# Value products behind the first query block's scores, in a causal attention with a mixture of experts behind it

## The chip, the core and the metric

One core of a Trainium2 chip runs one kernel. The metric is the device time of one execution in microseconds (us). The engines run side by side, each through its own list of instructions in order, and wait for one another on semaphores: TensorE (matmuls, PE in the profile, its weight loads PEld), VectorE (DVE), ScalarE (ACT), GpSimd (POOL) and SyncE (SP), which here only issues the DMAs.

## What is computed

The input x has 16 batches of 256 tokens with 128 features. Two layers follow each other, each added to its input:

```
x = x + attention(layernorm(x))     # 16 heads, keys of 8, values of 64, causal softmax
x = x + experts(layernorm(x))       # 8 experts, 64 tokens of each batch per expert
q = (x @ Wq), k = (x @ Wk), v = (x @ Wv);  scores = q k^T / sqrt(8), masked above the diagonal
ctx = softmax(scores) @ v;  attention = ctx @ Wo
probs = softmax(x @ gate_w); each expert takes its top 64 tokens: gelu(xin @ w1) @ w2, weighted, added back
```

All is float32. Where the kernel needs products close to float32 accuracy, it splits a factor into a rounded part ("hi") and a rest ("lo") and adds three faster products: hi x hi, hi x lo and lo x hi. `split_product` does this.

## The kernel before

The kernel has two stages, one after the other: `attention` and `experts`. The change is in `attention` alone.

Attention works in 64 units, u = 4b + j: batch b (16) times group j of four heads (4). I call j the unit of its batch, 0 to 3. Each engine has a function `batch(b, par)` with a loop over j, and in each pass of it the engine works on several units at different stages, so that the pass of unit u holds, on TensorE:

- L513, L515: the scores s1 of the second query block (tokens 128 to 255) of unit u+1, with the causal mask added by a matmul;
- L530, L531: eight transposes of the normalized probabilities of unit u-1 into the PSUM buffers t_ps, half f = 0 and half f = 1;
- L548: sixteen context matmuls of unit u-2 into ctx_ps, half as wide in the output's partitions as the others;
- L558: the value product of unit u+2 (three matmuls, L494 to L496), a quarter of the batch's values, into a buffer misc_ps;
- L565: four transposes of the last third of unit u-1's probabilities;
- L571, L572: the scores s0 of the first query block (tokens 0 to 127) of unit u+2;
- L584: the query and key products of unit u+3 (six matmuls, L494 to L496) into the other misc_ps buffer;
- then, into the misc_ps buffer that the value product used, one of four pieces of other work: the transposes of the normalized input xn1 (j = 0, L595), those of the second layer's xn2 (j = 1, L601), half of the output projection (j = 2, L606; its other half stands at L519 in unit 3), the gate's logits (j = 3, L610). Ahead of it TensorE waits for `v_ready`, ScalarE's copy of the value product out of that buffer (L591).

ScalarE copies the query and key product (L313, qk_hi), computes the exponentials of s0 (L317) and s1 (L330) with `exps`, four instructions each, and copies t_ps to probT (L323 for half 0, L341 for half 1) and the value product to v_sb (L337). VectorE makes qT and kT from qk_hi and the product (L409, L412), the negated maxima of s1 (L417) and s0 (L458), copies (L446, L479), the reciprocals, and the two layer normalizations: L394, called at L450 in unit 0 (xn1 of batch b+1) and at L455 in unit 1 (xn2 of batch b-2), two instructions of 128 tokens each. GpSimd spreads kT over four blocks of a diagonal (L266, `k_diag`, on which both score products wait through `k_ready`) and multiplies the probabilities by the reciprocal sums (L258 first query block, L281 second); in units 0 and 3 it has two small operations of the normalizations between L266 and L281 (L270 to L277).

The order of the work is written out by hand: it is the order of the `if` blocks in each engine's loop. There is no scheduler. `batches` writes the first and the last batches out and runs the middle ones in a loop.

Of the kernel before, what the change touches and what calls it, by code (L numbers as in the profile page):

```python
# [10 lines left out]
ACT = mybir.ActivationFunctionType  # L11
# [68 lines left out]
def attention(nc, x_tiles, w_q, w_k, w_v, w_o, gate_w, w1, w2,  # L80
# [5 lines left out]
    with ExitStack() as ctx:  # L86
# [201 lines left out]
        @block.scalar  # L288
        def _(act):

            act.wait_ge(wqk_loaded, 32)
            for w in range(2):
                nc.scalar.activation(wqk_hi[:, w, :, :, :],
                                     bcast(wqk_raw[:, w, :].rearrange("p (h d) -> p h d", h=H), 2, 4),
                                     ACT.Copy, scale=(DK ** -0.5 if w == 0 else 1.0)).then_inc(w_hi, 1)
            act.wait_ge(wv_loaded, 16)
            nc.scalar.activation(wv_hi[:, :], wv_raw[:, :], ACT.Copy).then_inc(w_hi, 1)

            def exps(r, block_, scores, keys, first, done):
                for i in range(HG):  # L300
                    last = nc.scalar.activation(  # L301
                        prob[r][:, first + i * keys:first + (i + 1) * keys], scores[:, i, :], ACT.Exp,
                        bias=neg_max[:, r, block_, i:i + 1], accum_out=sums[:, r, block_, i:i + 1])
                last.then_inc(done, 1)

            def batch(b, par):
                for j in range(G):
                    u = b * G + j
                    r1, r2, rm = (j + 1) % RING, j % RING, (j + 1) % RING
                    if has(u + 2, UNITS):  # L310
                        act.wait_ge(qk_done, u + 3)
                        await_count(act, qk_ready, u + 1)
                        nc.scalar.activation(qk_hi[r2][:, :, :],  # L313
                                             misc_ps[(3 * j) % 2][:, :].rearrange("p (a t) -> p a t", a=2),
                                             ACT.Copy).then_inc(qk_hi_done, 1)
                    if has(u + 1, UNITS):
                        act.wait_ge(max0, u + 2)  # L317
                        await_count(act, normed, u * 2)
                        exps(r1, 0, s0_ps, P, 0, exp0)
                    if has(u - 1, UNITS):  # L320
                        act.wait_ge(t_done, (u - 1) * 3 + 1)
                        await_count(act, ctx_done, u - 2)
                        nc.scalar.activation(probT[rm][:, 0:512], t_ps[rm][:, :], ACT.Copy).then_inc(t_act, 1)  # L323
                    if j == 1 and has(b + 1, B):
                        act.wait_ge(xT_done, b + 2)
                        nc.scalar.activation(xT_hi[1 - par][:, :], misc_ps[(3 * j + 1) % 2][:, 0:T],
                                             ACT.Copy).then_inc(xT_hi_done, 1)
                    if has(u + 1, UNITS):
                        act.wait_ge(max1, u + 2)
                        exps(r1, 1, s1_ps, T, HG * P, exp1)  # L330
                    if has(u + 2, UNITS):
                        w, q = u + 2, (j + 2) % G
                        vb = par if j < 2 else 1 - par
                        act.wait_ge(v_done, w + 1)

                        await_count(act, ctx_done, w - q - G)
                        nc.scalar.activation(v_sb[vb][:, q % 2, (q // 2) * 512:(q // 2 + 1) * 512],  # L337
                                             misc_ps[(3 * j) % 2][:, :], ACT.Copy).then_inc(v_ready, 1)
                    if has(u - 1, UNITS):
                        act.wait_ge(t_done, (u - 1) * 3 + 2)  # L340
                        nc.scalar.activation(probT[rm][:, 512:1024], t_ps[1 - rm][:, :], ACT.Copy).then_inc(t_act, 1)  # L341
                    if j == 2 and has(b - 2, B):
                        act.wait_ge(xn2_ready, b - 1)
                        nc.scalar.activation(xg_hi[:, bass.ds((b - 2) * TB, TB), :], xn2[:, :, :],
                                             ACT.Copy).then_inc(xg_hi_done, 1)

            batches(act, batch)
# [139 lines left out]
        def _(pe):  # L487
# [17 lines left out]
            def batch(b, par):  # L505
                for j in range(G):
# [26 lines left out]
                    if has(u - 2, UNITS):  # L533
# [15 lines left out]
                                                            v_sb[vb][:, kb, h * DV:(h + 1) * DV], rhs,  # L549
                                                            start=(kb == 0), stop=(kb == 1))  # L550
                        last.then_inc(ctx_done, 1)
                    if has(u + 2, UNITS):
                        w, q = u + 2, (j + 2) % G
                        xb = par if j < 2 else 1 - par
                        pe.wait_ge(qk_ready, w + 1)
                        toks = slice((q % 2) * P, (q % 2 + 1) * P)
                        cols = slice((q // 2) * 512, (q // 2 + 1) * 512)
                        split_product(misc_ps[(3 * j) % 2][:, :], xT_hi[xb][:, toks], xT_lo[xb][:, toks],  # L558
                                      wv_hi[:, cols], wv_lo[:, cols]).then_inc(v_done, 1)
                    if has(u - 1, UNITS):  # L560
                        w = u - 1
                        pe.wait_ge(t_act, w * 2 + 1)
# [4 lines left out]
                    if has(u + 2, UNITS):  # L567

                        pe.wait_ge(k_ready, u + 3)
                        await_count(pe, exp0, u + 2)  # L570
                        nc.tensor.matmul(s0_ps[:, :, :], qT[r2][:, 0:P], k_diag[r2][:, :, 0:P], start=True, stop=False)  # L571
                        nc.tensor.matmul(s0_ps[:, :, :], ident_bf[:, :], bcast(causal[:, :], 1, HG),  # L572
                                         start=False, stop=True).then_inc(s0_done, 1)
                    if has(u + 3, UNITS):
                        w, g = u + 3, (j + 3) % G
                        xb = par if j < 1 else 1 - par
                        heads = slice(g * HG, (g + 1) * HG)
                        qk_ps = misc_ps[(3 * j + 1) % 2]
                        pe.wait_ge(xT_ready, b + 1 if j < 1 else b + 2)

                        await_count(pe, *[(gate_ready, b - 2), (xT_ready, b + 2 if has(b + 1, B) else B), (x2T_ready, b - 1),
                                          (x1_ready, b)][j])
                        for a in range(2):
                            last = split_product(qk_ps[:, a * T:(a + 1) * T],  # L584
                                                 wqk_hi[:, a, heads, :, :].rearrange("p h r d -> p (h r d)"),
                                                 wqk_lo[:, a, heads, :, :].rearrange("p h r d -> p (h r d)"),
                                                 xT_hi[xb][:, :], xT_lo[xb][:, :])
                        last.then_inc(qk_done, 1)
# [361 lines left out]
```

## Time and profile before

| | us |
|---|---|
| median of 3 runs | 674.44 (673.14 to 677.0) |
| the profiled execution | 672.88 |
| its span, first to last instruction | 671.0 |
| TensorE busy | 591.7 (88%) |
| VectorE busy | 437.2 (65%) |
| ScalarE busy | 418.8 (62%) |
| GpSimd busy | 363.5 (54%) |

In the page's forty slices of the span (16.8 us each) TensorE is busy for nine tenths or more from the third to the twenty-sixth slice, which is attention; behind it come the routing and the experts, where TensorE has a gap and is then full again. The granted TensorE clock is 0.966 of full speed over the span, and full speed in the batches between 80 and 450 us. The DMA queues move 12.26 MB, most of it at the start and in the second stage. Busy times are sums of instruction times; a pipelined matmul's time overlaps the next one's, so distances between starts say more than durations there.

### The profile page before, as it was taken

To read this page: it belongs to the slowest core of one execution; us is meant where nothing else is said; L and a number is where in the kernel's file an instruction comes from. 1 tells how busy PE (TensorE), PEld (TensorE's weight loads), DVE (VectorE), ACT (ScalarE), POOL (GpSimd) and SP (SyncE) were. 2 spreads that over 40 slices of the span, in tenths; PEclk is the share of its full clock that TensorE was granted. 3 is DMA by queue.
4 is the path that set the end of the run, shared out by engine and by line. 5 is a ranking of instruction groups with operands and counts; after the bars stand their busy time and mean duration, and the time that the engine had idled before them with its cause. 6 is when DMAs were issued, how large, how long until landed. Compare 5 with 4: busy or idle time off the path is not lost. (4 is left out here: it accounts for less than half of the span.)

```text
span 671.0 us, 14745 instructions
## 1 busy us (share of the span) xinstructions
PE 591.7 (88%) x4996; PEld 482.5 (72%) x4996; DVE 437.2 (65%) x1072; ACT 418.8 (62%) x1418; POOL 363.5 (54%) x290
## 2 busy tenths in 40 slices
PE   1799999999999999999999999988408999999964
PEld 0467777878778777787877877766407989989863
DVE  3678787787887878878778787774475234433233
ACT  2699778787787877878778787773205443323320
POOL 1688778687776867768777687763240110111120
PEclk9999999999999999999999999999758999999995
DMA  9500000000000000000000000000001001000001
GB/s 275 172 1 1 2 1 1 1 3 1 1 0 0 0 0 0 0 0 0 0 0 0 0 0 1 1 0 2 0 32 48 17 18 31 11 17 18 17 17 40
DMA packets 13547, 12.26 MB, mean 18 GB/s; under 512 B 832, under 2 KB 10304, under 8 KB 13504
## 3 DMA queue, kind: packets, MB, share of 16 engines
q1 hardware_dynamic: 13504, 11.69, 5.9%
q8 instruction: 27, 0.44, 0.3%
q14 instruction: 16, 0.13, 0.1%
HBM read 9.57 MB, written 2.11 MB: 17 GB/s over the span
## 5 line engine op out<-in xcount | busy, mean ns | idle before, releaser
L301 ACT ACTIVATE prob<-s_ps,neg_max 128x128 f32<-128x128 f32 (+1 forms) x512 | 209.7, 433 | 36.4 <-DVE neg_max L417 20.4
L266 POOL TENSOR_TENSOR k_diag<-kT,own_block 128x1024 fp32r<-128x1024 f32 x64 | 121.3, 1895 | 111.0 <-DVE kT L412 111.0
L281 POOL TENSOR_TENSOR probn<-prob,inv 128x1024 f32<-128x1024 f32 x64 | 121.3, 1896 | 2.6 <-DVE inv L482 2.6
L301 ACT ACTIVATION_READ_ACCUMULATOR prob<-s_ps,neg_max 128x1 f32 x512 | 111.8, 218 | 0.0
L548 PE MATMUL ctx_ps<-probT,v_sb 128*64 128x256 f32 (+1 forms) x1024 | 97.3, 332 | 0.9 <-DVE probT L479 0.9
L737 POOL TENSOR_TENSOR y_parts<-y_sb,y_parts 128x512 fp32r<-128x512 f32 x16 | 20.9, 1306 | 140.4 <-ACT y_parts L753 140.4
L548 PEld LDWEIGHTS ctx_ps<-probT,v_sb 128*64 128x64 f32 x1024 | 63.6, 136 | 29.9 <-issue 11.6
L417 DVE TENSOR_REDUCE neg_max<-s_ps 128x4 f32<-128x1024 f32 x64 | 77.9, 1217 | 0.4 <-PE s_ps L515 0.4
L458 DVE TENSOR_REDUCE neg_max<-s_ps 128x4 f32<-128x512 f32 x64 | 44.1, 688 | 48.4 <-PE s_ps L572 48.4
L258 POOL TENSOR_TENSOR probn<-prob,inv 128x512 f32<-128x512 f32 x64 | 66.7, 1042 | 4.4 <-PE t_ps L565 4.1
L847 DVE TENSOR_TENSOR y_sb<-y_ps,slot_prob 128x512 f32<-128x512 f32 x16 | 11.1, 692 | 88.5 <-PE y_ps L925 88.5
L446 DVE COPY ctxT<-ctx_ps 128x512 f32<-128x512 f32 x64 | 43.9, 685 | 33.9 <-PE ctx_ps L548 32.8
L323 ACT ACTIVATE probT<-t_ps 128x512 f32<-128x512 f32 x64 | 39.1, 610 | 40.4 <-PE t_ps L531 40.4
L501 PE MATMUL misc_ps<-wo_sb,ctxT 128*128 128x128 f32 x512 | 63.8, 280 | 0.6 <-DVE xn2T L432 0.6
L530 PE MATMUL t_ps<-ident,probn 128*128 128x128 f32 x256 | 60.7, 277 | 1.4 <-DVE probT L479 1.0
L501 PEld LDWEIGHTS misc_ps<-wo_sb,ctxT 128*128 128x128 f32 x512 | 61.4, 196 | 0.8 <-issue 0.8
L531 PE MATMUL t_ps<-ident,probn 128*128 128x128 f32 x256 | 59.7, 273 | 0.0
L925 PE MATMUL y_ps<-w_sb,w_raw 128*64 128x128 f32 x1024 | 59.4, 274 | 0.0
L925 PEld LDWEIGHTS y_ps<-w_sb,w_raw 128*64 128x64 f32 x1024 | 55.6, 137 | 2.1
L761 ACT ACTIVATE xin_hi<-pick_hi_ps 128x512 fp32r<-128x512 f32 x16 | 9.6, 599 | 72.5 <-PE pick_lo_ps L884 72.5
L772 ACT ACTIVATE w_raw<-h_ps 128x512 f32<-128x512 f32 x64 | 38.2, 599 | 26.0 <-PE h_ps L905 23.7
L513 PE MATMUL s_ps<-k_diag,qT 128*128 128x512 f32 x128 | 53.0, 473 | 0.5 <-ACT v_sb L337 0.5
(127 smaller groups left out, 1403.6 us busy)
## 6 DMA issues: line engine op xcount, KB each, us to landing
x_all<-in_L_attn_x SPq DMA_DIRECT2D x4, 512.0 KB, 6.9
w_raw<-in_L_ffn_w SPq DMA_DIRECT2D x1, 2048.0 KB, 11.2
toks<-tok_rows SPq DMA_DIRECT2D x8, 256.0 KB, 3.1
out<-x_all SPq DMA_DIRECT2D x16, 128.0 KB, 1.8
wv_raw<-in_L_attn_Wv SPq DMA_DIRECT2D x1, 512.0 KB, 4.7
wo_sb<-in_L_attn_Wo SPq DMA_DIRECT2D x1, 512.0 KB, 5.8
wqk_raw<-in_L_attn_Wq SPq DMA_DIRECT2D x1, 64.0 KB, 3.5
wqk_raw<-in_L_attn_Wk SPq DMA_DIRECT2D x1, 64.0 KB, 3.5
```

The costliest lines, as they stand in the source:

```text
L258: nc.gpsimd.tensor_tensor(probn[r][:, 0:HG * P].rearrange("p (i k) -> p i k", i=HG), prob[r][:, 0:HG * P].rearrange("p (i k) -> p i k", i=HG),
L266: nc.gpsimd.tensor_tensor(k_diag[r][:, :, :], bcast(f32(kT[r][:, :]), 1, HG), bcast(own_block[:, :], 2, T), ALU.mult).then_inc(k_ready, 1)
L281: nc.gpsimd.tensor_tensor(probn[r][:, HG * P:].rearrange("p (i k) -> p i k", i=HG), prob[r][:, HG * P:].rearrange("p (i k) -> p i k", i=HG ...
L301: last = nc.scalar.activation(prob[r][:, first + i * keys:first + (i + 1) * keys], scores[:, i, :], ACT.Exp, bias=neg_max[:, r, block_, i: ...
L417: nc.vector.tensor_reduce(out=neg_max[:, r1, 1, :], in_=s1_ps[:, :, :], axis=AX.X, op=ALU.max, negate=True).then_inc(max1, 1)
L458: nc.vector.tensor_reduce(out=neg_max[:, r2, 0, :], in_=s0_ps[:, :, :], axis=AX.X, op=ALU.max, negate=True).then_inc(max0, 1)
L501: last = nc.tensor.matmul(to[:, tb * D:(tb + 1) * D], context[:, c, tb * P:(tb + 1) * P], wo_sb[:, c, :], start=(c == 0), stop=(c == chunk ...
L513: nc.tensor.matmul(s1_ps[:, i:i + 2, :], qT[r1][:, P:T], k_diag[r1][:, i:i + 2, :], start=True, stop=False)
L530: nc.tensor.transpose(t[:, i, 0:P], q0[:, 2 * f + i, :], ident[:, :])
L531: last = nc.tensor.transpose(t[:, i, P:T], q1[:, 2 * f + i, 0:P], ident[:, :])
L548: last = nc.tensor.matmul(ctx_ps[half * DV:(half + 1) * DV, pair, kb * P:T], v_sb[vb][:, kb, h * DV:(h + 1) * DV], rhs, start=(kb == 0), s ...
L925: last = nc.tensor.matmul(y_ps[half * CAP:(half + 1) * CAP, q, :], hT[m % RING][:, half, c, q * CAP:(q + 1) * CAP], w2_sb[:, 2 * (m % EP) ...
```

## The change

In TensorE's loop, the block with the value product moves behind two others: the four transposes L565 and the scores s0. It then stands directly ahead of the query and key products. In ScalarE's loop, the copy of t_ps half 1 into probT moves ahead of the copy of the value product. The semaphores and their counts stay as they are; VectorE, GpSimd and the DMAs are not touched.

```
 ScalarE, in batch():
                         exps(r1, 1, s1_ps, T, HG * P, exp1)
+                    if has(u - 1, UNITS):
+                        act.wait_ge(t_done, (u - 1) * 3 + 2)
+                        nc.scalar.activation(probT[rm][:, 512:1024], t_ps[1 - rm][:, :], ACT.Copy).then_inc(t_act, 1)
                     if has(u + 2, UNITS):
...
                         nc.scalar.activation(v_sb[vb][:, q % 2, (q // 2) * 512:(q // 2 + 1) * 512],
                                              misc_ps[(3 * j) % 2][:, :], ACT.Copy).then_inc(v_ready, 1)
-                    if has(u - 1, UNITS):
-                        act.wait_ge(t_done, (u - 1) * 3 + 2)
-                        nc.scalar.activation(probT[rm][:, 512:1024], t_ps[1 - rm][:, :], ACT.Copy).then_inc(t_act, 1)
 TensorE, in batch():
                         last.then_inc(ctx_done, 1)
+                    if has(u - 1, UNITS):
...
+                            last = nc.tensor.transpose(t[:, i, :], q1[:, i, P:T], ident[:, :])
+                        last.then_inc(t_done, 1)
+                    if has(u + 2, UNITS):
+
+                        pe.wait_ge(k_ready, u + 3)
+                        await_count(pe, exp0, u + 2)
+                        nc.tensor.matmul(s0_ps[:, :, :], qT[r2][:, 0:P], k_diag[r2][:, :, 0:P], start=True, stop=False)
+                        nc.tensor.matmul(s0_ps[:, :, :], ident_bf[:, :], bcast(causal[:, :], 1, HG),
+                                         start=False, stop=True).then_inc(s0_done, 1)
                     if has(u + 2, UNITS):
                         w, q = u + 2, (j + 2) % G
...
                         split_product(misc_ps[(3 * j) % 2][:, :], xT_hi[xb][:, toks], xT_lo[xb][:, toks],
                                       wv_hi[:, cols], wv_lo[:, cols]).then_inc(v_done, 1)
-                    if has(u - 1, UNITS):
...
-                        pe.wait_ge(k_ready, u + 3)
...
```

TensorE before, one pass in a unit 0, from the last context matmuls on (`wv`, `xT` into misc_ps0 is the value product, `ident`, `probn` the transposes, `k_diag`, `qT` and `causal` the scores s0, `wqk` the query and key products, `xn1` the work that reuses misc_ps0):

```order
L548 MATMUL ctx_ps<-probT0,v_sb0 64x128 x2
L494 MATMUL misc_ps0<-wv_hi,xT_hi1 128x512
L495 MATMUL misc_ps0<-wv_lo,xT_hi1 128x512
L496 MATMUL misc_ps0<-wv_hi,xT_lo1 128x512
L565 MATMUL t_ps1<-ident,probn1 128x128 x4
L571 MATMUL s0_ps<-k_diag0,qT0 128x512
L572 MATMUL s0_ps<-causal,ident_bf 128x512
L494 MATMUL misc_ps1<-xT_hi1,wqk_hi 128x256
L495 MATMUL misc_ps1<-xT_lo1,wqk_hi 128x256
```

The same place of the changed kernel, in which L557 is what L565 was, and L563 and L564 are what L571 and L572 were:

```order
L548 MATMUL ctx_ps<-probT0,v_sb0 64x128 x2
L557 MATMUL t_ps1<-ident,probn1 128x128 x4
L563 MATMUL s0_ps<-k_diag0,qT0 128x512
L564 MATMUL s0_ps<-causal,ident_bf 128x512
L494 MATMUL misc_ps0<-wv_hi,xT_hi1 128x512
L495 MATMUL misc_ps0<-wv_lo,xT_hi1 128x512
L496 MATMUL misc_ps0<-wv_hi,xT_lo1 128x512
L494 MATMUL misc_ps1<-xT_hi1,wqk_hi 128x256
L495 MATMUL misc_ps1<-xT_lo1,wqk_hi 128x256
```

The three value matmuls have moved past six others and stand last but one group ahead of the work that reuses their buffer.

ScalarE before, one pass from the exponentials of s1 on:

```order
L301 ACTIVATE prob1,sums<-s1_ps,neg_max 128x256 x4
L337 ACTIVATE v_sb0<-misc_ps0 128x512
L341 ACTIVATE probT1<-t_ps0 128x512
L313 ACTIVATE qk_hi1<-misc_ps1 128x512
L301 ACTIVATE prob0,sums<-s0_ps,neg_max 128x128 x4
```

The same place of the changed kernel (L333 is what L341 was, L340 what L337 was):

```order
L301 ACTIVATE prob1,sums<-s1_ps,neg_max 128x256 x4
L333 ACTIVATE probT1<-t_ps0 128x512
L340 ACTIVATE v_sb0<-misc_ps0 128x512
L313 ACTIVATE qk_hi1<-misc_ps1 128x512
L301 ACTIVATE prob0,sums<-s0_ps,neg_max 128x128 x4
```

The two copies have changed places; what stands around them is as before.

## Rows read from the trace of the kernel before

**Rows 1.** Busy time (instructions) by engine in one batch; then clock, DMA share, GB/s.

```profile
299.59:327.53 27.94, 27.20 (x214) 21.52 (x214) 22.20 (x55) 22.16 (x83) 20.69 (x16) 1.00 0.00 0
```

**Rows 2.** TensorE's waits, 50 to 450 us: us in total, times, longest.

```profile
PE misc_ps L601 <- issue: 5.5, 7, 0.8
PE misc_ps L601 <- DVE xn L394: 4.6, 6, 0.8
```

**Rows 3.** Timeline of TensorE, unit 3: start, us, engine, line, what, number.

```profile
324.76 0.50 PE L494 MATMUL misc_ps<-wv_hi,xT_hi 128*128 128x512 f32 x1
...
325.33 0.40 PE L496 MATMUL misc_ps<-wv_hi,xT_lo 128*128 128x512 f32 x1
...
325.56 0.60 PE L565 MATMUL t_ps<-ident,probn 128*128 128x128 f32 x4
...
327.05 0.28 PE L496 MATMUL misc_ps<-xT_hi,wqk_lo 128*128 128x256 f32 x1
...
327.17 0.51 PE L610 MATMUL misc_ps<-gate_sb,xn2T 128*128 128x8 f32 x4
```

**Rows 4.** Timeline of ScalarE in the same unit.

```profile
325.76 0.60 ACT L337 ACTIVATE v_sb<-misc_ps 128x512 f32<-128x512 f32 x1 [0.36 <-PE misc_ps L496]
...
327.45 0.60 ACT L313 ACTIVATE qk_hi<-misc_ps 128x512 fp32r<-128x512 f32 x1 [0.60 <-PE misc_ps L496]
```

**Rows 5.** Timeline of several engines in an early unit.

```profile
25.80 0.61 ACT L337 ACTIVATE v_sb<-misc_ps 128x512 f32<-128x512 f32 x1
...
26.32 0.60 ACT L313 ACTIVATE qk_hi<-misc_ps 128x512 fp32r<-128x512 f32 x1
...
26.46 0.49 PE L513 MATMUL s_ps<-k_diag,qT 128*128 128x512 f32 x1 [0.18 <-ACT v_sb L337]
...
26.95 0.48 DVE L409 SCALAR_TENSOR_TENSOR qT<-qk_hi,minus_low,misc_ps 128x256 fp32r<-128x256 f32 x1 [0.56 <-ACT qk_hi L313]
...
27.91 1.89 POOL L266 TENSOR_TENSOR k_diag<-kT,own_block 128x1024 fp32r<-128x1024 f32 x1 [1.18 <-DVE kT L412]
```

**Rows 6.** Timeline of GpSimd, VectorE and TensorE, unit 0.

```profile
329.59 1.90 POOL L266 TENSOR_TENSOR k_diag<-kT,own_block 128x1024 fp32r<-128x1024 f32 x1 [2.31 <-DVE kT L412]
...
331.49 0.59 DVE L394 TENSOR_SCALAR xn<-x_all,mv,rstd 128x128 f32 x2
...
332.37 1.90 POOL L281 TENSOR_TENSOR probn<-prob,inv 128x1024 f32<-128x1024 f32 x1
...
333.24 0.43 PE L595 MATMUL misc_ps<-ident,xn 128*128 128x128 f32 x2
```

**Rows 7.** The same engines in unit 1.

```profile
337.07 1.90 POOL L281 TENSOR_TENSOR probn<-prob,inv 128x1024 f32<-128x1024 f32 x1
...
337.61 2.44 DVE L394 TENSOR_SCALAR xn<-x_all,mv,rstd 128x128 f32 x2
...
338.93 1.04 POOL L258 TENSOR_TENSOR probn<-prob,inv 128x512 f32<-128x512 f32 x1
...
340.15 0.41 PE L601 MATMUL misc_ps<-ident,xn 128*128 128x128 f32 x2 [0.79 <-issue]
```

**Rows 8.** VectorE and GpSimd in the experts' stage.

```profile
645.82 0.35 DVE L853 TENSOR_SCALAR place<-col_no,slot_tok 128x256 fp32r<-128x256 bf16 x1
...
645.86 1.43 POOL L737 TENSOR_TENSOR y_parts<-y_sb,y_parts 128x512 fp32r<-128x512 f32 x1 [5.26 <-ACT y_parts L753]
```

**Rows 9.** GpSimd and TensorE in unit 2.

```profile
342.17 1.90 POOL L266 TENSOR_TENSOR k_diag<-kT,own_block 128x1024 fp32r<-128x1024 f32 x1 [2.20 <-DVE kT L412]
...
344.70 0.47 PE L571 MATMUL s_ps<-k_diag,qT 128*128 128x512 f32 x1
```

**Rows 10.** TensorE in the first units.

```profile
18.87 0.79 PE L571 MATMUL s_ps<-k_diag,qT 128*128 128x512 f32 x1 [0.32 <-POOL k_diag L266]
...
24.85 0.50 PE L571 MATMUL s_ps<-k_diag,qT 128*128 128x512 f32 x1 [1.01 <-POOL k_diag L266]
...
31.88 0.41 PE L595 MATMUL misc_ps<-ident,xn 128*128 128x128 f32 x2 [0.58 <-DVE xn L394]
```

More of the change, by code:

```diff
@@ L551, in batch @@
                         last.then_inc(ctx_done, 1)
[L552 to L559, printed above, removed]
                     if has(u - 1, UNITS):
@@ L573, in batch @@
                                          start=False, stop=True).then_inc(s0_done, 1)
+                    if has(u + 2, UNITS):
+                        w, q = u + 2, (j + 2) % G
+                        xb = par if j < 2 else 1 - par
+                        pe.wait_ge(qk_ready, w + 1)
+                        toks = slice((q % 2) * P, (q % 2 + 1) * P)
+                        cols = slice((q // 2) * 512, (q // 2 + 1) * 512)
+                        split_product(misc_ps[(3 * j) % 2][:, :], xT_hi[xb][:, toks], xT_lo[xb][:, toks],
+                                      wv_hi[:, cols], wv_lo[:, cols]).then_inc(v_done, 1)
                     if has(u + 3, UNITS):
```

## Prediction

> **What bounds the kernel now.** I read the windows first, then TensorE's waits, then the timeline of one batch on all engines. Attention fills the first two thirds of the span, and in its middle every batch takes the same 27.9 us. In one such batch TensorE is busy for 27.20 of 27.94 us and no other engine for more than 22.2 [rows 1]. The reader is to see that TensorE streams nearly without a gap: what is added to its order, or makes it wait, lengthens the batch. Its waits between 50 and 450 us come to about 11 us, and nearly all of that is one place, L601, the transpose of xn2 in unit 1 of a batch: 5.5 + 4.6 us over 13 batches, 0.78 each [rows 2]. So at most 10 us can be won by ordering; the other places have no wait to remove.
>
> Why L601 waits decides much here. VectorE's two L394 instructions of unit 1 take 2.44 us from 337.61, where the two of unit 0 take 0.59 [rows 6, 7]. They run beside GpSimd's L281 and L258. The pair ends 0.08 us behind the end of L258 (338.93 + 1.04 = 339.97; 337.61 + 2.44 = 340.05), the transpose follows at 340.15 [rows 7]. A normalization that starts once a large GpSimd product has started waits for the whole product. In unit 0 the pair falls into the gap between k_diag's end and L281, in which GpSimd has only the two small operations from L275 on, so it is free [rows 6].
>
> **The change, part by part.** TensorE's instructions are the same in number; only their order changes. VectorE and GpSimd keep theirs, and no DMA moves.
>
> *The first scores come earlier.* A value product costs TensorE 0.23 us per instruction (325.33 to 325.56), so 0.7 for three [rows 3]. Transposes and s0 now start 0.7 to 0.8 us earlier, if the keys are ready. VectorE's maximum L458, which waits for s0, and all queued behind it come forward. In unit 3 that queue is what makes qT late, and k_diag with it: qk_hi starts at 327.45 and k_diag at 329.59, 2.14 us later [rows 4, 6]. Where VectorE was free, qT started 0.63 behind qk_hi (26.32 to 26.95) and k_diag 0.96 behind qT (27.91) [rows 5]. With the queue gone I take these: k_diag at 327.45 + 0.63 + 0.96 = 329.04 instead of 329.59, and L281, 2.78 behind it (329.59 to 332.37 [rows 6]), at 331.82 instead of 332.37. By itself that is no gain: it keeps TensorE from waiting at s0, which it now reaches 0.7 us earlier.
>
> *The value product comes late for its copy.* At the end of each unit TensorE waits for v_ready before it writes to the misc_ps buffer that the value product used. From the start of the last value matmul: it ends 0.40 later, the copy starts 0.03 behind (325.33 + 0.40 = 325.73, copy at 325.76 [rows 3, 4]), takes 0.60, and TensorE reacts 0.05 later (copy 25.80 + 0.61 = 26.41, matmul at 26.46 [rows 5]): 1.08 us. TensorE itself now has only the q/k product in between: 0.23 and six steps of 0.12 (327.05 to 327.17 [rows 3]), 0.94. So it waits 0.14, say 0.15, at the end of units 0, 2 and 3; before, transposes and s0 filled 0.7 us more and it had no such wait. In unit 1 it lies under the L601 wait. The swap on ScalarE costs nothing: the second transposed half was done long before, and the value copy couldn't start any sooner than the product ends. If ScalarE came out of the exponentials late, the wait would grow by up to the 0.60 of the copy that now stands ahead; I take 0.15, bounds 0 and 0.75.
>
> *The normalization of unit 0 loses its gap.* This term decides. The 0.15 at the end of unit 3 pushes TensorE's context product of unit 0 and with it VectorE's L394 pair from 331.49 to 331.64. A free tile alone takes about 0.35 (as L853's [rows 8]) and the pair 0.59, so the second starts some 0.25 behind the first, at 331.89. L281 now starts at 331.82, 0.07 earlier. What happens at such distances: an L853 started 0.04 before an L737 (645.82 and 645.86) ran free in its usual 0.35 and the GpSimd product took 1.43 [rows 8]; the second L394 of unit 1 starts 0.05 behind L258 and waits all of it [rows 7]. The border lies between 0.04 ahead and 0.05 behind; my 0.07 behind is on the wrong side by little. Blocked, the tile is ready at 331.82 + 1.90 + 0.08 = 333.80, and the transpose L595 starts at 333.90 instead of 333.24: +0.65.
>
> The Trainium skill, SBUF — State Buffer, section "Who interferes with whom", says that issue order decides who gets the port pair shared by VectorE and GpSimd, and that the other blocks fully. The waits of rows 7 agree with it. By that rule the border is at equal starts, which makes the blocked case a little likelier than the rows alone do; had the two engines shared the port instead, the tile would be late by tenths and this term would be near nothing.
>
> *Units 1 and 2 behind it.* From the end of the normalization to the next k_diag is 2.12 us (340.05 to 342.17 [rows 7, 9]). In unit 1 k_diag then starts at 333.80 + 2.12 = 335.92, L281 1.85 behind it (the step from one large product to the next, 337.07 to 338.93) at 337.77 instead of 337.07 [rows 7], and L258, the second normalization and L601 are all 0.70 later: the 0.78 wait of L601 absorbs nothing, because its cause moves with it. In unit 2, k_diag is ready 2.12 + 1.90 + 0.05 = 4.07 behind the normalization's end; before, s0 started 4.65 behind it (344.70 [rows 9]), now it could at 3.95. It waits 0.12, and with the value product of 0.7 behind it the rest of the unit is 4.07 + 0.70 - 4.65 = 0.12 later. Then 0.15 of v_ready in unit 2. Behind the half-width context matmuls the first value matmul takes longer: two steps are 0.57 (324.76 to 325.33) where 2 x 0.23 would be 0.46 [rows 3]. The transposes are first now and gave up less in my estimate, half of that 0.11: -0.05 in unit 3. Per batch: 0.70 + 0.12 + 0.15 - 0.05 = 0.92 us.
>
> The gap of unit 0 exists in 13 batches (the two small operations come with b-2, so not in the first ones, and the last batch normalizes nothing): 13 x 0.92 = 12.0 us.
>
> *The start.* In the first units TensorE waits for k_diag before s0, 0.32 us in the first, 1.01 in the second and as much again in the third, with the value product ahead of that wait, as filler [rows 10]. It is now behind, in the chain q/k product, copy, qT, k_diag, s0: 0.9 for the first (partly at the slower pace of that stretch), 0.7 to 0.8 for each of the next two, about 0.5 for the fourth: +3.0. About 0.8 comes back, in the 0.58 that L595 waits at 31.88 [rows 10] and in short waits of unit 4 and 5: +2.2, bounds 0.5 and 3.5. The second stage is not touched.
>
> Sum: 672.88 (the profiled execution, 671.0 span and 1.9 around it) + 12.0 + 2.2 = 687.1. The median of the three runs before is 1.56 higher, 674.44, so I forecast 688.6.
>
> **The rivals.**
> - *The second tile still gets in ahead of L281.* For it: 0.07 us is a small distance, and the latencies I added vary by 0.05. Against: the v_ready wait has to be under 0.04 for it. Then the end of the second normalization is about 0.12 earlier (L258 follows a kT which is 0.2 earlier, less the wait), and the batch is -0.12 + 0.12 + 0.15 - 0.05 = +0.10: 1.3 + 2.2 = 3.5 us, 678.
> - *Not slower but faster: the earlier keys shorten the L601 wait.* Place: unit 1. GpSimd's chain k_diag, L281, L258 starts up to 0.23 earlier because L281 of unit 0 is out of its way, L601 goes with it, and 58 units save 0.05 each at the context's end. 13 x 0.23 + 2.9 = 5.9, less the 2.2 of the start: 3.7 gained, 670.7. It decides if TensorE never waits for v_ready and k_diag of unit 2 is ready at 3.95 behind the normalization. Against it stand 1.08 against 0.94 and 4.07 against 3.95. At the very most the whole of L601's 10 us goes: 666.6.
> - *Nothing but the start.* All small terms cancel: 674.4 + 2.2 = 676.6. For it: TensorE has the same work and was 97% busy.
>
> **How the numbers follow.** Blocked tile 0.58 (own range 684 to 692, from 0.8 to 1.05 per batch and the bounds of the start), tile free 0.22, only the start 0.10, faster 0.10. About 0.5%, 3.4 us, is what a measurement can tell from no change: 671.0 to 677.8 is "same". The blocked case is all slower (0.58); the free tile lies at the border (0.11 slower, 0.11 same); only the start is mostly same (0.01 slower, 0.08 same, 0.01 faster); the faster one is 0.03 same and 0.07 faster. Slower 0.70, same 0.22, faster 0.08. Range 675 to 692: it leaves out the faster rival and the upper tail.
>
> **What would show it.** In the profile after, steady batches of 28.8 us; L394 of unit 0 at 2 to 2.2 us for the pair and L595 waiting for it about 0.6; L458 waiting less for s0; L610 and L501 of TensorE waiting 0.15 for the value copy; s0 with a short wait for k_diag in unit 2. Wrong would be: L394 at 0.59 in unit 0 (then 678 at most), or TensorE's waits at L601 below 0.5 (then the faster rival). If waits for the value copy are far above 0.15, ScalarE is the bound that I priced too low.

## The result and the profile after

| | before | after |
|---|---|---|
| median | 673.79 (4 runs, 672.86 to 677.0) | 697.25 (4 runs, 696.45 to 699.33) |
| ratio, 95% interval | | 1.034 [1.031, 1.0371] |
| span of the profiled execution | 671.0 | 695.0 |
| mean granted clock | 0.966 | 0.958 |

The kernel is slower by 23.5 us, 3.4%. I had forecast 14.2 more, so the direction is right and the time is above my range. The two traces split the 24.0 us between their spans by the start of L513, which stands at the head of each pass. The first instructions on x come 0.36 later in this execution, which is chance; until batch 2's first L513 (it starts at 68.68 before, 75.25 after) another 6.2 are lost; the stretch from there to the last L513 lasts 383.21 before and 400.57 after, 17.35 more; the second stage is the same within 0.1. I had put 2.2 on the start and 12.0 on the steady part.

The steady part first: two whole batches of the profile after, in windows. The columns are those of [rows 1]: length, then busy us of PE, PEld, DVE, ACT, POOL.

```profile
338.30:367.36 29.06, 27.74 (x216) 21.70 (x214) 24.01 (x54) 22.48 (x83) 20.67 (x16) 1.00 0.00 0
308.24:338.30 30.06, 27.95 (x216) 21.78 (x214) 24.82 (x54) 22.57 (x83) 20.67 (x16) 1.00 0.00 0
```

There are two kinds of batch. Eight of the twelve from batch 3 to batch 14 take 29.06 to 29.16, four take 29.8 to 30.1; in [rows 1] it was 27.94. The mean is 29.37 against 27.90. VectorE is busier by 1.8 to 2.6 us with the same instructions: blocked time shows as busy time. TensorE's waits between 50 and 450 us (us in total, times, longest), the answer to [rows 2]:

```profile
PE misc_ps L595 <- DVE xn L394: 9.8, 13, 1.3
PE misc_ps L601 <- issue: 5.9, 7, 0.8
PE misc_ps L601 <- DVE xn L394: 4.7, 6, 0.8
```

L601 waits as before; L595, the transposes in unit 0, waited once before (0.8 us) and now waits in every batch. The weight loads of TensorE (PEld), same stretch:

```profile
PEld s_ps L563 <- POOL k_diag L266: 3.8, 21, 0.2
PEld misc_ps L501 <- ACT v_sb L340: 2.4, 13, 0.2
PEld misc_ps L610 <- ACT v_sb L340: 2.2, 12, 0.2
```

These are the stops for the value copy that I had forecast (0.2 each, in units 2 and 3) and the short wait of s0 for its keys. Unit 0 of a short batch, the answer to [rows 6] (start, us, engine, line, what):

```profile
347.67 1.89 POOL L266 TENSOR_TENSOR k_diag<-kT,own_block 128x1024 fp32r<-128x1024 f32 x1 [2.31 <-DVE kT L412]
...
350.20 2.22 DVE L394 TENSOR_SCALAR xn<-x_all,mv,rstd 128x128 f32 x2
...
350.45 1.89 POOL L281 TENSOR_TENSOR probn<-prob,inv 128x1024 f32<-128x1024 f32 x1
...
352.48 0.44 PE L595 MATMUL misc_ps<-ident,xn 128*128 128x128 f32 x2 [0.48 <-DVE xn L394]
```

The pair starts 0.25 ahead of L281, the first tile runs free, the second (0.25 behind the first, so level with L281) waits out the product: 2.22 us where [rows 6] had 0.59. And unit 0 of a long batch:

```profile
320.31 3.05 DVE L394 TENSOR_SCALAR xn<-x_all,mv,rstd 128x128 f32 x2
320.39 1.89 POOL L281 TENSOR_TENSOR probn<-prob,inv 128x1024 f32<-128x1024 f32 x1
...
323.42 0.44 PE L595 MATMUL misc_ps<-ident,xn 128*128 128x128 f32 x2 [1.31 <-DVE xn L394]
```

Here the pair is listed 0.08 ahead of L281, and both tiles wait. Unit 1, the answer to [rows 7], is of the old kind; the pair is a little nearer to L281's start (0.21 behind it instead of 0.54), so it is blocked longer but not later:

```profile
356.40 1.89 POOL L281 TENSOR_TENSOR probn<-prob,inv 128x1024 f32<-128x1024 f32 x1
...
356.61 2.75 DVE L394 TENSOR_SCALAR xn<-x_all,mv,rstd 128x128 f32 x2
...
359.47 0.41 PE L601 MATMUL misc_ps<-ident,xn 128*128 128x128 f32 x2 [0.84 <-issue]
```

The stop for the value copy in unit 3, timeline of TensorE, the answer to [rows 3]:

```profile
314.67 0.40 PE L496 MATMUL misc_ps<-wv_hi,xT_lo 128*128 128x512 f32 x1
...
315.49 0.28 PE L496 MATMUL misc_ps<-xT_hi,wqk_lo 128*128 128x256 f32 x1
315.75 0.61 PE L610 MATMUL misc_ps<-gate_sb,xn2T 128*128 128x8 f32 x4
316.36 0.49 PE L513 MATMUL s_ps<-k_diag,qT 128*128 128x512 f32 x1
```

From the last value matmul to L610 it is 1.08, as I had worked out. What I had not: from L610 to L513 it was 0.36 in every batch before. Here it is 0.47, and 0.58 to 0.66 in the passes like this one, where the branch between two rounds of the loop falls behind L610.

The start, the answer to [rows 10] (TensorE):

```profile
19.23 0.80 PE L563 MATMUL s_ps<-k_diag,qT 128*128 128x512 f32 x1 [3.56 <-POOL k_diag L266]
...
26.34 0.80 PE L563 MATMUL s_ps<-k_diag,qT 128*128 128x512 f32 x1 [2.86 <-POOL k_diag L266]
27.02 0.99 PE L494 MATMUL misc_ps<-wv_hi,xT_hi 128*128 128x512 f32 x1
...
28.66 0.42 PE L494 MATMUL misc_ps<-xT_hi,wqk_hi 128*128 128x256 f32 x1
...
33.71 0.80 PE L563 MATMUL s_ps<-k_diag,qT 128*128 128x512 f32 x1 [2.23 <-POOL k_diag L266]
...
41.09 0.50 PE L563 MATMUL s_ps<-k_diag,qT 128*128 128x512 f32 x1
```

The first four s0 come 7.1 to 7.4 us apart; before they stood at 18.87, 24.85, 29.85 and 35.20, 5.0 to 6.0 apart. The value product between s0 and the q/k product takes 28.66 - 27.02 = 1.64. Windows of both kernels, clock in the third column from the end, before first:

```profile
25.00:30.00 5.00, 3.37 (x16) 2.02 (x16) 3.82 (x8) 4.33 (x20) 3.79 (x4) 1.00 0.19 51
30.00:35.00 5.00, 4.42 (x29) 3.27 (x29) 4.64 (x7) 4.56 (x20) 4.40 (x3) 1.00 0.00 2
35.00:40.00 5.00, 4.51 (x35) 3.30 (x36) 3.59 (x9) 4.81 (x20) 4.09 (x4) 1.00 0.02 5
```

```profile
25.00:30.00 5.00, 3.66 (x12) 2.99 (x12) 1.30 (x4) 2.53 (x9) 3.13 (x4) 0.57 0.21 59
30.00:35.00 5.00, 2.77 (x8) 1.46 (x8) 4.18 (x6) 3.92 (x17) 3.23 (x2) 0.50 0.00 0
35.00:40.00 5.00, 5.00 (x23) 4.10 (x22) 2.83 (x6) 2.73 (x11) 2.37 (x3) 0.56 0.01 2
```

After, TensorE runs at the lower of its two levels (1.2 GHz) from about 25.7 to 39 us; it fell during the wait of 2.86, in which TensorE stood idle; before, it stays at the upper one. Its 23 matmuls between 35 and 40 us fill the window that 35 did not fill before.

### The profile page after: what moved, and what is told of

It reads as the page before. It is cut to its first block and busy times, and to the rows that moved or that the text cites. A ratio compares the mean times of both kernels' runs of the same rounds, so it can differ in the third digit from the quotient of the medians.

```text
span 695.0 us, 14745 instructions
## 1 busy us (share of the span) xinstructions
PE 603.6 (87%) x4996; PEld 489.1 (70%) x4996; DVE 462.4 (67%) x1072; ACT 424.5 (61%) x1418; POOL 363.4 (52%) x290
## 5 line engine op out<-in xcount | busy, mean ns | idle before, releaser
L281 POOL TENSOR_TENSOR probn<-prob,inv 128x1024 f32<-128x1024 f32 x64 | 121.4, 1896 | 2.6 <-DVE inv L482 2.6
L301 ACT ACTIVATION_READ_ACCUMULATOR prob<-s_ps,neg_max 128x1 f32 x512 | 107.1, 209 | 0.0
L394 DVE TENSOR_SCALAR xn<-x_all,mv,rstd 128x128 f32 (+1 forms) x64 | 75.2, 1215 | 2.2 <-POOL rstd L272 1.2
L501 PE MATMUL misc_ps<-wo_sb,ctxT 128*128 128x128 f32 x512 | 63.6, 278 | 0.6 <-DVE xn2T L432 0.6
L501 PEld LDWEIGHTS misc_ps<-wo_sb,ctxT 128*128 128x128 f32 x512 | 59.6, 192 | 3.4 <-ACT v_sb L340 2.5
L925 PE MATMUL y_ps<-w_sb,w_raw 128*64 128x128 f32 x1024 | 61.1, 279 | 0.0
L925 PEld LDWEIGHTS y_ps<-w_sb,w_raw 128*64 128x64 f32 x1024 | 57.2, 140 | 2.2
L513 PE MATMUL s_ps<-k_diag,qT 128*128 128x512 f32 x128 | 54.5, 485 | 0.4 <-ACT v_sb L340 0.3
```

The source lines that it names most:

```text
L281: nc.gpsimd.tensor_tensor(probn[r][:, HG * P:].rearrange("p (i k) -> p i k", i=HG), prob[r][:, HG * P:].rearrange("p (i k) -> p i k", i=HG ...
L301: last = nc.scalar.activation(prob[r][:, first + i * keys:first + (i + 1) * keys], scores[:, i, :], ACT.Exp, bias=neg_max[:, r, block_, i: ...
L394: last = nc.vector.tensor_scalar(dst[:, tb, :], src(tb), mv[:, tb, 0:1], rstd[:, tb:tb + 1], ALU.subtract, ALU.mult)
L501: last = nc.tensor.matmul(to[:, tb * D:(tb + 1) * D], context[:, c, tb * P:(tb + 1) * P], wo_sb[:, c, :], start=(c == 0), stop=(c == chunk ...
L513: nc.tensor.matmul(s1_ps[:, i:i + 2, :], qT[r1][:, P:T], k_diag[r1][:, i:i + 2, :], start=True, stop=False)
L925: last = nc.tensor.matmul(y_ps[half * CAP:(half + 1) * CAP, q, :], hT[m % RING][:, half, c, q * CAP:(q + 1) * CAP], w2_sb[:, 2 * (m % EP) ...
```

## The experiments

All were timed beside the kernel before, whose median was 672.63, 674.49 and 673.56 in the three sets of rounds; a ratio refers to its own set, so a difference between the medians of two versions can carry 1 to 2 us of that. "Batch" is the mean of batches 3 to 14 in the trace, "pass" the distance from one L513 to the next, named by its unit. Where GpSimd is held, this line stands ahead of its wait for the reciprocals (L281), for j = 0, 1 or both:

```
 # GpSimd's loop
+if j == 0 and has(b + 1, B): pool.wait_ge(xn1_ready, b + 2)
+if j == 1 and has(b - 2, B): pool.wait_ge(xn2_ready, b - 1)
 pool.wait_ge(inv1, u + 1)      # then L281
```

It lets VectorE finish the normalization before L281 may start, so no tile is blocked in that unit.

**1. Each half of the change alone.** TensorE's move with ScalarE's order of before:

```
 # ScalarE: value copy first, then transposed half 1, as before
 # TensorE: transposes, s0, value product, q/k product, as after
```

> The changed kernel with ScalarE's order as before: only TensorE's value product is moved. Theory (order on TensorE does all of it): ScalarE reaches the value copy before the product has ended in units 0 and 3, so the copy of the transposed half waits behind it, which costs nothing, because the context product needs it only a unit later: 697, within 1.5 us of the changed kernel. Rival (the swap on ScalarE delays the value copy in some units and is part of the loss): 690 or less, since in units 1 and 2 the value copy would come up to 0.5 us sooner.

Measured 692.18 (691.12 to 692.62), ratio 1.0289 [1.0265, 1.0313]; batch 28.85, and these alternate between 28.5 and 29.25. Two of its unit 0 pairs:

```profile
259.41 2.29 DVE L394 TENSOR_SCALAR xn<-x_all,mv,rstd 128x128 f32 x2
259.72 1.90 POOL L281 TENSOR_TENSOR probn<-prob,inv 128x1024 f32<-128x1024 f32 x1
...
288.56 0.59 DVE L394 TENSOR_SCALAR xn<-x_all,mv,rstd 128x128 f32 x2
289.00 1.91 POOL L281 TENSOR_TENSOR probn<-prob,inv 128x1024 f32<-128x1024 f32 x1
```

0.31 ahead of L281 only the first tile gets through, 0.44 ahead both do. Neither the 697 that I expected nor the rival's 690 was met. So some of the loss needs the swap on ScalarE, which I had priced at nothing: 5.1 us by the medians, 3.4 by the ratios, 5.8 by the spans of the two traces. And which batches are short is a matter of 0.1 us.

ScalarE's swap with TensorE's order of before:

```
 # ScalarE: transposed half 1 first, then value copy, as after
 # TensorE: value product, transposes, s0, q/k product, as before
```

> The kernel before with the two ScalarE copies swapped and nothing else. Theory: on TensorE the value product still ends 1.6 us ahead of the work that reuses its buffer; in units 0 to 2 ScalarE comes out of the exponentials late, and the copy 0.5 us later is then ready about 0.4 us too late in unit 0 and 0.1 too late in unit 2, so 5 to 7 us slower than before: 679 to 681. Rival (the swap is free): 674.

Measured 678.63 (678.33 to 680.84), 1.0096 [1.0067, 1.0125]; batch 28.29. The pair of unit 0 runs free; the price is this wait of TensorE (50 to 450 us):

```profile
PE misc_ps L595 <- ACT v_sb L340: 5.0, 13, 0.5
```

As expected, within 0.4 us. The halves add up to 18.4 + 4.8 = 23.2 us (by the ratios to 3.9%, where both together cost 3.4%), but not because they are independent: the next group shows that.

**2. The blocked tiles taken away.** The changed kernel with GpSimd held in unit 0:

> The changed kernel with one wait more: in unit 0 of a batch GpSimd waits for the normalization xn1 before it starts the large product L281. Theory (the normalization, blocked behind L281, is what makes unit 0 long): the two L394 of unit 0 take 0.6 us again, TensorE's wait at L595 goes, unit 0 falls from 6.68 to about 6.1 us (0.15 of it the wait for the value copy), 13 batches give 8 to 10 us back: 688. Rival (unit 0 is long because of the value copy): L595 waits as long for v_ready, 696 or more.

Measured 682.13 (681.8 to 684.46), 1.0148 [1.0118, 1.0178]; batch 28.29, pass of unit 0 6.04 instead of 6.68, and unit 1 6.51 instead of 6.95, which I had not expected. Blocking in unit 0 alone costs 29.37 - 28.29 = 1.08 us per batch, its largest single part.

The kernel before with GpSimd held in unit 1, where [rows 7] had its only large wait:

> The kernel before, with one wait more: in unit 1 GpSimd waits for the normalization xn2 before it starts the large product L281. Theory (what makes TensorE wait 0.78 us at L601 is VectorE's normalization blocked behind GpSimd's products): the L394 pair of unit 1 takes 0.6 instead of 2.44 us, L281 starts 1.1 later and is still done before TensorE's transposes need it, TensorE's wait at L601 goes, 13 batches x 0.8 = 10 us: 663. Rival (GpSimd is too full to give 1.1 us away in that unit): the wait moves to L530, and it is 672 to 676.

Measured 661.95 (661.67 to 662.79), 0.9821 [0.9785, 0.9857]: faster than both kernels. Unit 1:

```profile
276.47 0.59 DVE L396 TENSOR_SCALAR xn<-x_all,mv,rstd 128x128 f32 x2
277.15 1.89 POOL L283 TENSOR_TENSOR probn<-prob,inv 128x1024 f32<-128x1024 f32 x1 [1.16 <-DVE xn L396]
...
278.07 0.38 PE L603 MATMUL misc_ps<-ident,xn 128*128 128x128 f32 x2
```

The same instruction as in [rows 7] takes 0.59 for 2.44, L603 (L601 there) waits no longer, and GpSimd, which waited 1.16 for it, has the time.

The changed kernel held in both units:

> The changed kernel with GpSimd waiting for the normalizations in units 0 and 1. Theory: against the run with the wait in unit 0 alone (682.1), TensorE's wait at L601 (about 0.6 us per batch) goes as well, but the wait for the value copy, now 1.1 us behind the product, takes its place for 0.15: 5 us less, 677. What is left over the kernel before with its wait in unit 1 is the start (5 us), the wait for the value copy and its refill (0.25 in each of units 0 to 3, 1.0 per batch, 13 us): that difference should be 12 to 16 us. Rival (only the blocked normalizations cost): the difference is 5.

Measured 671.73 (671.03 to 673.99), 0.9962 [0.9944, 0.998]. With no tile blocked on either side, the change costs 9.8 us instead of 23.5, between my 12 to 16 and the rival's 5. In the traces it is 5.2 at batch 2 and 6.2 from there to the last L513. By passes (us):

| | unit 3 | unit 0 | unit 1 | unit 2 | batch |
|---|---|---|---|---|---|
| before | 7.77 | 5.90 | 6.90 | 7.33 | 27.90 |
| after | 8.02 | 6.68 | 6.95 | 7.73 | 29.37 |
| before, held in 1 | 7.77 | 5.91 | 5.91 | 7.49 | 27.08 |
| after, held in 0 and 1 | 8.01 | 6.05 | 5.99 | 7.52 | 27.56 |

Holding GpSimd gives back 0.82 per batch before and 1.81 after. I take these as what blocking costs, 0.99 more after; the rest of the change is 27.56 - 27.08 = 0.48.

The last one with ScalarE's two copies in the old order:

> TensorE's changed order with ScalarE's old order of the two copies, and GpSimd held until the normalization is through in units 0 and 1, as in the kernel that gave 671.7 with both parts of the change. Theory: the swap on ScalarE costs time only because it shifts L281 against the tiles; with the tiles free it costs nothing: 670.5 to 673. Rival (the swap has a price of its own, the 4 to 5 us that it cost without the waits): 667 to 668.

Measured 673.75 (672.63 to 675.43), 1.0003 [0.9993, 1.0013]; batch 27.59. The rival is wrong, though the time lies 0.75 above my range: with TensorE's new order and no tile blocked, the swap costs nothing, and undoing it gains nothing (its first L513 came 0.55 later than in the version with it, which makes part of the 2.0 us between them). So the 5 us of experiment 1 are blocking too. How it comes about stands in ScalarE's rows of a unit 3, first TensorE's move alone, then the changed kernel:

```profile
283.50 0.60 ACT L337 ACTIVATE v_sb<-misc_ps 128x512 f32<-128x512 f32 x1 [1.22 <-PE misc_ps L496]
284.00 0.59 ACT L341 ACTIVATE probT<-t_ps 128x512 f32<-128x512 f32 x1
284.47 0.60 ACT L313 ACTIVATE qk_hi<-misc_ps 128x512 fp32r<-128x512 f32 x1
```

```profile
345.14 0.60 ACT L340 ACTIVATE v_sb<-misc_ps 128x512 f32<-128x512 f32 x1 [0.72 <-PE misc_ps L496]
345.94 0.60 ACT L313 ACTIVATE qk_hi<-misc_ps 128x512 fp32r<-128x512 f32 x1 [0.20 <-PE misc_ps L496]
```

In the old order the copy of the transposed half stands between the value copy and the copy of the q/k product, which starts 0.97 behind the value copy; in the new order it is out of the way, and it is 0.80. The keys, k_diag and L281 follow: k_diag starts 286.22 - 284.62 = 1.60 and L281 289.00 - 284.62 = 4.38 behind the L513 that heads that unit 0, against 1.41 and 4.19 in the changed kernel (347.67 and 350.45 behind 346.26), while the pair starts 3.94 behind it in both. With the old order L281 is 0.2 later, and the pair gets through in every second batch.

**3. The loop's branch.** Why are some batches long and some short? The middle batches run two to a round of a loop. The changed kernel with that loop written out:

```
-with engine.Fori(2, (B - 2) // 2) as pair:
-    for k in range(2):
-        batch(pair * 2 + k, k)
+for b in range(4, B - 2):
+    batch(b, b % 2)
```

> The changed kernel with the loop over pairs of batches written out, so that no engine branches. In the changed kernel batches of 29.06 us alternate with some of 29.8 to 30.1, and the long ones follow a unit 3 in which TensorE's branch stands behind its wait for the value copy. Theory (the branch, 0.2 us, is exposed by the new wait and makes both tiles of the normalization late): all batches are 29.1, unit 3 is 7.97, 3 to 4 us less: 693. Rival (the alternation comes from the phase of GpSimd and VectorE): batches of 29.8 remain and the time is the same, 697.

Measured 702.43 (701.65 to 704.22), 1.0421 [1.038, 1.0463]: slower, where I had expected a gain. The theory that the branch makes the long batches is wrong; it is the other way round. Written out, every batch is a long one, 29.82 to 29.84, and every unit 0 looks like this:

```profile
294.19 2.99 DVE L393 TENSOR_SCALAR xn<-x_all,mv,rstd 128x128 f32<-128x128 f32 x2
294.20 1.89 POOL L280 TENSOR_TENSOR probn<-prob,inv 128x1024 f32<-128x1024 f32 x1
```

Undisturbed, the changed order settles with the pair level with L281; in the kernel with the loop, where the branch delays TensorE in every second batch, it is knocked out of that.

The kernel before, written out in the same way:

> The kernel before with the loop over pairs of batches written out, as was done to the changed kernel, where it made every batch 29.83 us with both tiles blocked. Theory: in the kernel before the pair of unit 0 lies well inside its gap, so shifts of 0.2 us by the loop's branch decide nothing: 672 to 676, batches 27.8 to 27.9. Rival (the gap is as delicate there): over 680, batches of 28.5 or more.

Measured 673.59 (672.69 to 676.79), 1.0009 [0.9993, 1.0025], batches 27.84 to 27.85. As expected: there the pair starts 0.85 to 0.98 ahead of L281, and 0.2 us either way do nothing.

**4. The start.** The changed kernel with TensorE's old order in the written-out passes up to batch 0 alone:

```
+early = isinstance(b, int) and b < 1
+if has(u + 2, UNITS) and early:      # value product at its old place
 ...                                  # transposes, s0
-if has(u + 2, UNITS):
+if has(u + 2, UNITS) and not early:  # value product at its new place
```

> The changed kernel, but TensorE's passes of the first three batch steps (the written-out passes up to batch 0) have the value product where it was before; from batch 1 on the order is the changed one. Theory (start costs 6.6 us, because TensorE waits longer for the keys without the value product as filler, and its clock then falls to half for 13.7 us): the clock stays full from 21 us on, and 6 us come back: 691. Rival (my first sum: the start costs 2.2): 695.

Measured 694.74 (693.31 to 696.62), 1.0328 [1.0295, 1.036]. Batch 2 begins at 70.49 instead of 75.25, with x 0.35 later: 5.1 gained. By the last L513 it is 4.2, since one batch more is of the long kind, and at the end of the profiled run only 2.6: its second stage took 1.6 longer, which I can't explain. By the time alone the rival's 695 is met and not my 691: what speaks against the rival is the start of batch 2, and the second stage, which is the same in all these kernels, varies between 218.1 and 221.5 us over their traces, as much as theory and rival differ by. The opposite, the new order in those passes alone (ScalarE's swap throughout):

```
+early = not (isinstance(b, int) and b < 1)
```

> TensorE's changed order and ScalarE's new order of the two copies; TensorE goes back to the order of before from batch 1 on, so the changed order holds in the start alone. Theory: the start costs what the two traces show at batch 2, 6 us, of which some comes from the half clock between 25 and 40 us, and nothing of it is given back later. ScalarE's order stays the new one, as in the kernel in which it was swapped alone (678.6). So 683 to 685, and batch 2 begins near 75. Rival (the 2.2 us of my forecast, the half clock being hidden under waits): 680 to 681, batch 2 near 71.

Measured 682.68 (680.93 to 685.7), 1.0127 [1.011, 1.0144]. Against the version with the swap alone, 678.63, the start costs 4.05 us by the medians, 3.1 when each is set against the kernel before of its own rounds, 2.1 by the ratios; their traces give 74.31 - 69.92 = 4.4 at batch 2, 0.3 of it the arrival of x. Its steady batches are the same (28.28 and 28.29). The time is a little under my 683 to 685 and over the rival's 680 to 681, but it doesn't settle the 2.2; the start of batch 2 does. Over all fourteen traces, batch 2 begins 63.9 to 66.1 us behind the first instruction on x in the seven kernels whose start has TensorE's new order, and 59.1 to 60.5 in the seven others; and the clock falls to the lower level between 25 and 40 us in each of the seven and in none of the others. This run also shows what the clock does. Here the second value product still ran at the upper level, the third no longer (TensorE):

```profile
26.79 0.51 PE L572 MATMUL s_ps<-k_diag,qT 128*128 128x512 f32 x1 [2.23 <-POOL k_diag L266]
27.18 0.58 PE L494 MATMUL misc_ps<-wv_hi,xT_hi 128*128 128x512 f32 x1
...
28.07 0.28 PE L494 MATMUL misc_ps<-xT_hi,wqk_hi 128*128 128x256 f32 x1
...
32.88 0.79 PE L572 MATMUL s_ps<-k_diag,qT 128*128 128x512 f32 x1 [2.23 <-POOL k_diag L266]
```

From s0 to s0 it is 6.09 with the value product at 0.89 and 7.38 where it takes 1.64 (26.34 to 33.71 in the changed kernel: 7.37). So in a unit at the lower level the pace costs 1.3 us; the order alone costs up to 6.09 - 5.00 = 1.1 against the same unit before (24.85 to 29.85); up to, because part of this q/k product was already slow.

**5. A third place for the value product**, between the transposes and s0, with ScalarE's new order:

```
 transposes (L557)
+value product
 s0 (L563)
-value product
 q/k product
```

> The changed kernel, but on TensorE the value product stands between the transposes and the scores s0, so that it fills the wait for the keys again and has 0.35 us more in front of the work that reuses its buffer. Theory: no wait for the value copy where ScalarE is free, the normalization of unit 0 keeps its gap, the clock stays full at the start; left is what the swap on ScalarE costs, up to 6 us: 675 to 679. Rival (s0 ahead of the value product is what made GpSimd's L281 early, and 0.36 us earlier is enough for that): 688 or more.

Measured 678.51 (677.89 to 682.06), 1.0077 [1.0047, 1.0106]; batch 28.23, tiles free in unit 0. The start is as before (batch 2 at 69.20). With GpSimd held in both units:

> The value product between the transposes and s0 of the first half, ScalarE's new order, and GpSimd held in units 0 and 1. Against the version without the held GpSimd (678.5) the blocked pair of unit 1 goes, 0.8 to 1.2 us per batch: 663 to 668. The theory on the rest of the change (0.48 us per batch that blocking doesn't explain comes from TensorE's stop for the value copy, because only the q/k product is left in between) expects it nearer to 663, since s0 now stands between too and the start is as before. Rival (the 0.48 comes from ScalarE's order): 668 or more.

Measured 664.81 (663.51 to 665.38), 0.9866 [0.985, 0.9883], within the range given; batch 27.33. It loses 0.25 per batch to the kernel before held in unit 1, and one line of its TensorE waits carries more than that:

```profile
PE misc_ps L599 <- ACT v_sb L344: 5.6, 13, 0.5
```

Of the 0.48 per batch of the changed order, half goes when s0 stands behind the value product again. That fits the stop for the copy as its cause and does not prove it: the wait that is left sits in unit 0, for the value copy, and the kernel with the swap alone has the same wait (5.0).

## Why the prediction was wrong in size and right in direction

Two terms of the sum were too small. Per batch I had 0.92 us, and it was 29.37 - 27.90 = 1.47: 0.99 for blocked tiles where I had 0.70, since I counted on one blocked tile where in four of twelve batches it was both, and 0.48 for the rest where I had 0.22. And the start took 6.2 us where I had 2.2, since I priced the value product at the pace of the upper clock level. Together that is 17.35 + 6.2 for 12.0 + 2.2.

**The first scores and the keys: right, with luck.** k_diag and L281 of unit 0 keep their distance of 2.78 (347.67 to 350.45), and L281 came nearer to the pair, as forecast. But I had put the whole approach down to VectorE's queue. With TensorE's move alone the pair is still 0.44 or 0.31 ahead of L281, and in half the batches both tiles are free; the last 0.2 came from the swap on ScalarE.

**The normalization of unit 0 loses its gap: right in kind, too small.** I had the second tile 0.07 behind L281 and blocked, and L595 waiting about 0.6. In the short batches it is level with L281 and L595 waits 0.48; a short batch is about 1.2 us longer than before. What I missed is the first tile. I took the border from [rows 8], where a VectorE instruction 0.04 ahead of a GpSimd one ran free. Here a tile 0.08 ahead is blocked. The two cases differ in more than one way, and no run tells which counts: there GpSimd had idled for 5.26 us, here L281 follows another GpSimd operation directly; and L853 is another instruction (bf16 in, 256 wide), of which no trace shows one blocked, since none starts inside a large GpSimd product. I had put 0.18 between the first tile and L281 and never asked what happens if it shrinks. In four of the twelve batches from batch 3 to batch 14 it did: 0.3 per batch over all. (I had counted 13; in batch 2 the pair still stood 0.46 ahead and ran free.) The blocked tiles cost 0.99 per batch more than before, my terms for them (0.70) too little by 0.29.

The Trainium skill, SBUF — State Buffer, section "Who interferes with whom", has whoever issues first take the port pair for its whole instruction while the other blocks fully. That it is all or nothing the rows bear out (the pair of unit 0 takes 0.59, about 2.2 or about 3.0 us, and nothing in between). Read off the listed starts, though, the rule would have freed the first tile of the long batches, 0.08 us ahead; the measurement decides, and the listed start is not the moment of the lock.

**Units 1 and 2: right in kind, unit 2 too small.** The wait of L601 moved with its cause and absorbed nothing (0.84 for 0.79). Unit 1 is 0.05 longer, as I had it, unit 2 0.40, for which I had 0.12 + 0.15.

**The value copy: the stop was right, its consequences weren't counted.** 1.08 from value matmul to L610 or L501, as worked out. But the stop cost more than its wait: L610 to L513 grew from 0.36 to 0.47, and to 0.58 to 0.66 where the loop's branch falls behind it; before, the branch made no difference there. With all tiles free the order costs 0.48 per batch, 0.23 of it in unit 3, where I had 0.10, and 0.14 in unit 0. My terms for all this come to 0.22 (0.12 + 0.15 - 0.05). For unit 3 the runs bear out both parts: in the changed kernel with its loop written out the distance is 0.47 in every batch, and in experiment 5, with s0 behind the value product, it is 0.36 again. What the rest of the 0.26 is made of, in units 0 and 1 above all, no run isolates.

**The swap on ScalarE: wrongly reasoned.** With TensorE's new order and free tiles it costs nothing, as the last run of group 2 says; but it set where L281 stands against the pair, and is worth 5 us of blocking. With TensorE's old order it has a price of its own, 28.29 - 27.90 = 0.39 per batch, with L595 waiting 0.4 for the value copy. I had looked only at who waits for the two copies, not at the copy of the q/k product behind them, which starts sooner.

**The start: the largest miss in proportion, 6.2 for 2.2.** Undone alone it gives back 5.1 at batch 2, done alone it costs 4.1; the rest is what batch 1 already loses like any other. I priced a value product in the chain at 0.7 to 0.9, its pace at the upper level. It took 1.64 three times, and the q/k product was slower with it. The first time TensorE was at the slower pace before as well; the other two fall in the stretch in which the clock had dropped behind the longer waits. My upper bound of 3.5 fell with the same assumption: it allowed for the order and not for the clock.

**The rivals.** "Tile free" held in the changed kernel only in batch 2; it is half of the first experiment. "Faster" died with the blocked tile. "Only the start" named a real term and left out the larger one.

## What to carry to other kernels

Where VectorE and GpSimd alternate, read each pair's distance to the next large GpSimd operation, of every tile and not of the last alone, and count a tile forecast within some tenths of a microsecond of it as undecided, whatever an instruction elsewhere in the trace did: 0.08 ahead was blocked here and 0.10 ran free, and my forecast of the distance (0.18) was off by up to 0.1. A wait that keeps GpSimd back until VectorE is through can be worth more than a better order: here it gave 1.8% to the kernel before. And filler work that is moved behind a wait lengthens the wait; in a start-up phase, price it also at the lower clock.

## What the hardware showed beyond expectation

- **The border of the block is not at equal listed starts.** Over the traces of the changed kernel and its variants, a tile listed 0.00 to 0.08 us ahead of L281 is blocked. At 0.10 to 0.13 ahead it ran free and L281 took 1.96 to 1.99 instead of 1.89:

```profile
262.07 2.17 DVE L394 TENSOR_SCALAR xn<-x_all,mv,rstd 128x128 f32 x2
262.19 1.97 POOL L281 TENSOR_TENSOR probn<-prob,inv 128x1024 f32<-128x1024 f32 x1
```

- **The order settles in the bad case by itself.** The written-out kernel has the pair 0.00 to 0.02 us ahead of L281 in each of its steady batches, where both tiles are blocked; the one of before, 0.85 ahead, stays there. What holds it at 0.01 looks like a feedback between the engines, which I haven't traced.
- **The granted clock's record and the pace can disagree.** In the run held in unit 0 the window gives 1.00 (third column from the end), yet the matmuls ran at the pace of the changed kernel's 0.50 (0.99 for the first):

```profile
26.00:28.00 2.00, 1.82 (x4) 1.31 (x5) 0.53 (x1) 1.26 (x6) 1.92 (x4) 1.00 0.04 13
```

```profile
26.87 0.99 PE L496 MATMUL misc_ps<-wv_hi,xT_hi 128*128 128x512 f32 x1
```

The Trainium skill, TensorE: Matmul & The Clock Gate, Part 1, warns that the trace's clock events have been seen to be unreliable; these two rows agree. The distance between matmul starts is the surer reading.
